# Standardisation of the second graph layer: x in pieces of 2, 4, 8 and 12 tiles, and the order of the mean's sum

## The reference, cut to what matters

```python
def _L1_gnn_ref(node_feats, adj_matrix, W, b):
    adj = adj_matrix + jnp.eye(n, dtype=adj_matrix.dtype)
    deg = jnp.sum(adj, axis=1)
    dinv = jnp.where(deg > 0, deg ** (-0.5), 0.0)
    adj_norm = dinv[:, None] * adj * dinv[None, :]
    x = node_feats @ W.T + b
    mean = jnp.mean(x, axis=0, keepdims=True)
    std = jnp.std(x, axis=0, ddof=1, keepdims=True)
    x = (x - mean) / (std + 1e-06)
    return adj_norm @ x

x = x + _L1_gnn_ref(_layernorm(x, axis=-1), adj, L1_gnn_W, L1_gnn_b)
```

## Time and profile before

| | |
|---|---|
| median of three runs | 1944.17 us |
| profiled execution | 1942.8 us |
| its span, first to last instruction | 1941.0 us |
| mean granted TensorE clock | 0.973 |
| TensorE busy | 1790.1 us (92%) |
| VectorE busy | 1619.5 us (83%) |
| ScalarE busy | 1327.9 us (68%) |
| GpSimd busy | 964.0 us (50%) |
| standardisation, first load issued | 828.90 us from the span's start |
| mean read by VectorE | 875.24 us |
| first matmul of the contraction | 879.57 us |

### The profile page before, as it was taken

One profiled execution on the slowest core, in us unless ns is written; L12 is line 12 of the kernel. 1 busy time (PEld: TensorE's weight loads), 2 busy tenths in 40 slices (PEclk: granted clock), 3 DMA queues, 4 the chain that ended last, 5 costly groups with the idle time before them and its releaser, 6 DMA issues. The chain is left out here.

```text
span 1941.0 us, 41693 instructions
## 1 busy us (share of the span) xinstructions
PE 1790.1 (92%) x12628; PEld 1683.5 (87%) x12628; DVE 1619.5 (83%) x4235; ACT 1327.9 (68%) x2651; POOL 964.0 (50%) x1703
## 2 busy tenths in 40 slices
PE   5789999739999999869999979999999999999997
PEld 4578999739999999857888869999999999999997
DVE  5799877639999999748665559999999999999996
ACT  4334555326666666444555459999999999999995
POOL 2000145535555555440101127777777777777774
PEclk9999999859999999979999999999999999999999
DMA  8776779147888888443656400000000000000002
GB/s 295 245 257 196 220 197 203 59 145 229 238 230 228 233 236 236 115 166 118 196 171 203 136 12 2 2 2 2 2 2 2 2 2 2 2 2 2 2 2 72
DMA packets 97235, 226.26 MB, mean 117 GB/s; under 512 B 20897, under 2 KB 51363, under 8 KB 88620
## 3 DMA queue, kind: packets, MB, share of 16 engines
q1 hardware_dynamic: 82476, 206.33, 34.1%
q0 software_dynamic: 14592, 17.91, 4.8%
HBM read 204.43 MB, written 19.75 MB: 115 GB/s over the span
## 5 line engine op out<-in xcount | busy, mean ns | idle before, releaser
L2036 PE MATMUL ffn_psH<-ffn_w2h,ffn_vTh 128*128 128x256 f32 x1320 | 391.8, 297 | 1.5 <-DVE ffn_u L2092 1.5
L2036 PE MATMUL ffn_psH<-ffn_w2h,ffn_vTl 128*128 128x256 f32 x1320 | 373.2, 283 | 0.0
L2036 PE MATMUL ffn_psH<-ffn_w2l,ffn_vTh 128*128 128x256 f32 x1320 | 372.8, 282 | 0.0
L2125 POOL TENSOR_SCALAR ffn_vn<-ffn_vn,ffn_rstd,ffn_shift 128x256 f32<-128x256 f32 x540 | 299.8, 560 | 21.1 <-issue 1.2
L2080 DVE BATCH_NORM_STATS2 ffn_stats<-ffn_vn 128x6 f32<-128x256 f32 x780 | 285.2, 408 | 25.1 <-ACT ffn_vn L2062 24.0
L2092 DVE SCALAR_TENSOR_TENSOR ffn_u<-ffn_th,ffn_psH 128x512 f32<-128x512 f32 x390 | 264.3, 678 | 7.3 <-ACT ffn_th L2059 7.3
L2036 PEld LDWEIGHTS ffn_psH<-ffn_w2h,ffn_vTh 128*128 128x128 f32 x1320 | 252.1, 191 | 2.5 <-DVE ffn_u L2092 1.7
L2036 PEld LDWEIGHTS ffn_psH<-ffn_w2l,ffn_vTh 128*128 128x128 f32 x1320 | 252.4, 191 | 0.8
L2036 PEld LDWEIGHTS ffn_psH<-ffn_w2h,ffn_vTl 128*128 128x128 f32 x1320 | 251.7, 191 | 0.0
L2062 ACT ACTIVATE ffn_vn<-ffn_u 128x512 f32<-128x512 f32 x390 | 248.6, 637 | 0.8 <-DVE ffn_u L2092 0.8
L2059 ACT ACTIVATE ffn_th<-ffn_psH 128x512 f32<-128x512 f32 x390 | 232.8, 597 | 1.6 <-PE ffn_psH L1999 1.6
(11 more groups left out here) (242 smaller groups left out, 4992.1 us busy)
## 6 DMA issues: line engine op xcount, KB each, us to landing
g_raw<-in_adjt SPq DMA_DIRECT2D x168, 384.0 KB, 4.6
g_raw<-in_wide SPq DMA_DIRECT2D x78, 512.0 KB, 4.3
moe_w1raw<-in_wall SPq DMA_DIRECT2D x33, 1024.0 KB, 5.2
moe_w2raw<-in_wall SPq DMA_DIRECT2D x33, 1024.0 KB, 5.9
moe_b<-in_eb SPq DMA_DIRECT2D x33, 128.0 KB
g_raw<-in_adjl SPq DMA_DIRECT2D x14, 256.0 KB, 2.7
g_raw<-in_narrow SPq DMA_DIRECT2D x13, 256.0 KB, 2.7
xn_rows<-rt_hn SPq DMA_DIRECT2D x8, 384.0 KB, 4.4
```

What stands on the lines that cost most here:

```text
L2036: last = pe.matmul(psH[w % R][:, q * D:(q + 1) * D], a[:, w % R, q * KD + k, :], b[:, k, :], start=(k == 0 and j == 0), stop=(k == KD - 1 ...
L2125: last = pool.tensor_scalar(vn[:, t, :], vn[:, t, :], rstd[:, s:s + 1], shift[:, s:s + 1], ALU.mult, ALU.add)
```

## The change

The table of pieces becomes 2, 4, 8 and 12 tiles instead of 6, 8, 6 and 6. VectorE runs the statistics of the first three pieces ahead of all z, and those of the fourth behind z of group 1. TensorE's sum of the mean begins with the two halves of GpSimd's total and ends with the last group's two tiles; the waits move with them.

```diff
@@ -1032,7 +1032,7 @@
     def __init__(self, sb, sem, g, x_rows, w1, b1, z, squares, banks, lent):
         Q = 2
         G = NT // Q
-        LOADS = ((0, 6), (6, 14), (14, 20), (20, NT))
+        LOADS = ((0, 2), (2, 6), (6, 14), (14, NT))
         B = 3
         b = sb("std_b", [P, D])
         stats = sb("std_stats", [P, NT, 6])
@@ -1088,15 +1088,15 @@
                 dve.wait_ge(aggr_done, k + 1)
                 dve.tensor_scalar(veps[:, first:end], mv[:, first:end, 1], LN_EPS, None, ALU.add).then_inc(eps_done, 1)
 
-            statistics(0)
-            statistics(1)
+            for k in range(3):
+                statistics(k)
             dve.wait_ge(w_loaded, 32)
             for k in range(G):
                 dve.wait_ge(mm_done, k + 1)
                 dve.tensor_tensor(z[:, group(k), :], psZ[k % B], b[:].unsqueeze(1).broadcast_to([P, Q, D]),
                                   ALU.add).then_inc(z_done, 1)
-                if k in (0, 2):
-                    statistics(2 + k // 2)
+                if k == 1:
+                    statistics(3)
             dve.wait_ge(sum_done, 1)
             dve.tensor_scalar(mean[:], psM, 1.0 / N, None, ALU.mult).then_inc(mean_done, 1)
             dve.wait_ge(mean_done, 1)
@@ -1177,13 +1177,13 @@
                                              stop=(d == KD - 1))
                     last.then_inc(mm_done, 1)
 
+            pe.wait_ge(total_done, G - 2)
+            for q in range(Q):
+                pe.matmul(psM, g.ones[:], total[:, q, :], start=(q == 0), stop=False)
             pe.wait_ge(z_done, G)
             for q in range(Q):
-                pe.matmul(psM, (g.ones if q < Q - 1 else g.valid)[:], z[:, (G - 1) * Q + q, :], start=(q == 0),
-                          stop=False)
-            pe.wait_ge(total_done, G - 2)
-            for q in range(Q):
-                last = pe.matmul(psM, g.ones[:], total[:, q, :], start=False, stop=(q == Q - 1))
+                last = pe.matmul(psM, (g.ones if q < Q - 1 else g.valid)[:], z[:, (G - 1) * Q + q, :], start=False,
+                                 stop=(q == Q - 1))
             last.then_inc(sum_done, 1)
 
         def add_squares(pe, k):
```

## The result

The changed kernel took 1949.34 us (median of 7 runs, 1945.50 to 1952.54), the kernel before 1943.80 us (7 runs, 1940.29 to 1945.23). The ratio is 1.0028, with a 95% interval of 1.0017 to 1.0038: 5.5 us slower (the interval is 3.3 to 7.4 us), at the upper end of the stated range, 1943.8 to 1949.4. It lies outside the forecast's own range of 1945.2 to 1948.1, and beyond the likeliest case (+2.7) by about as much as that case itself.

The account below looks back on a forecast made before the run. TensorE was taken to bound the second graph layer, then a serial handover: 3.1 us late from the last piece, less 0.4 from the sum's order, gives +2.7 on 1944.17, so 1946.9 us; range 1943.8 to 1949.4.

Parts of the forecast that it names:

- forecast's own range: Whole kernel: +1.0 to +3.9 us, 1945.2 to 1948.1, from the unknown ends; a landing off by up to 2.8 goes beyond it.
- likeliest case: Whole kernel: TensorE's pause makes it +2.7 us slower, 1946.9 us; chance 0.52.
- What bounds the stage, and the last piece: Second graph layer: TensorE bounds it; the 12-tile piece's late statistics make TensorE wait 3.4 us, group 7's transposes 3.1 late.
- central forecast: Second graph layer: TensorE waits for the 12-tile piece, 3.1 us late, less 0.4 from the mean's sum: +2.7 us; chance 0.52.
- The head: Start of the second graph layer: first transposes at least 1.6 us earlier, but groups 3 to 6 stay; group 3 gains up to 0.6.
- Where the pieces land: Loads of x: tiles 6 to 13 again there at 839.05, shift 0, far end 2.8 us either side.
- The clock: TensorE's granted clock: a pause of 3.4 us can go either way, falling to half or staying full.
- Rival (1): TensorE behind the new pause: restarts at half clock, 1.5 to 2.7 us on top, +4.2 to +5.4 in all; chance 0.27.
- The sum: TensorE's sum of the mean: totals first, behind GpSimd's last addition, which waits for group 11's bias add; gains 0.4 us.
- The sum against the run: Whole kernel: +2.7 us on the three runs' median of 1944.17 gives 1946.9; the profiled execution would go from 1942.8 to 1945.5.

## Why the prediction was right, and where it was short

- **What bounds the stage, and the last piece.** The chain from z1 to T7 was put at 9.9 us and measured 9.90 (848.68 to 858.58); its parts were 0.61, 5.16 for the statistics, 0.09, 2.27 for the power, 0.59 for the two operations behind it and 1.18 for ScalarE's rows, each within 0.02 of the forecast but the last, which was put at 1.09; the forecast's terms add up to 9.81 and were rounded up on the way, so that the sums agree to 0.01 is luck. The pause came to 3.43 for 3.4, in front of T7 and ended by ScalarE. Moving the statistics alone takes it away and brings L back to 46.62. That was the mechanism of the central forecast, and it is shown.
- **The head ("costs nothing, gives nothing").** This step was mis-sized by +0.92: T7 was forecast 30.0 after the first load (858.9 less 828.90) and came at 30.92. T3 was to gain 0.6, as if M0 would come sooner. The 4-tile piece was taken to land by 837.0, 8.1 after the first load, and it did, at 8.13; but its rows then passed statistics, power and ScalarE, so T2 was at 14.48 instead of 13.49, and with it M0. T0 came 4.1 us earlier, as forecast, and that bought nothing. The four profiles of the changed kernel's pieces have T3 at 18.66 to 19.30, and the one taken here is the lowest, so +0.92 is rather the low end of this term. The step looked at groups 3 to 6 and took M0, which hangs on groups 1 and 2, as free to move ahead.
- **Where the pieces land ("I take 0, as the bytes ahead are unchanged").** The 8-tile piece came 0.68 later with the same bytes ahead. Order counts, not only bytes: 10.83 to 12.02 in the four profiles of the new pieces against 9.42 to 10.15 in three of the old ones, and 9.74 against 7.90 and 8.12 with b moved in both. So b's load isn't the reason for the difference between the orders; the small pieces' low rate goes with it, and its cause is open. All lie within the stated 2.8 of the old landing.
- **The clock.** Rival (1), given 0.27, is what this profile shows: the fall at 859.5, 1.73 lost, inside the 1.5 to 2.7. In one thing it differs: TensorE restarted at full level, and the fall came 0.9 to 1.4 us into T7's work. The unread products give 1.68 of it back. The Trainium skill's warning on gaps between matmul bursts ("TensorE: Matmul & The Clock Gate", section "Why this matters for your kernels") agrees with the trace here, with 1.7 us as its price; the 4.07 us of the first layer had made it look less likely than it was. That pause was an exception: over the ten profiles the same pause is 2.44 to 4.83 us long, and the clock falls in it or within a microsecond behind it in eight; only in the kernel before (4.07) and in the changed kernel (2.51) it doesn't. The pauses of 3.43 in the changed kernel and 3.42 in the run with b late both ended in a fall, and so did all eight of 4.36 ahead of the contraction without unread products. As far as the profiles show, 0.27 was too low. How often it falls in the runs without a profile is open: of them only a mean is known.
- **The sum.** -0.4 forecast, -0.38 and -0.39 measured. Its cover was as said: GpSimd's last addition waited for z11. Take the late z away, as with two pieces of 6, and the same order loses about 1.1 against the old one.
- **The sum against the run.** 2.7 + 0.92 + 1.73 = 5.35, and L grew by 5.36. The median's +5.5 fits that; the terms behind the mean (-0.9, +1.2) are the clock's scatter, and together nearly nothing. The central forecast's +2.7 lies below the measured interval (3.3 to 7.4): what came is that forecast, rival (1) and a head that cost where nothing was put. The chances had 0.69 for a difference within 3.9 us and 0.27 for a larger loss, which is what the medians show. The number came inside the stated range by 0.06 us, because the range reached up to rival (1); with runs from 1945.50 to 1952.54 that is luck, and the mechanism is not.

## What to carry to other kernels

When a stream is cut into unequal pieces, the chain behind the largest one must fit into the work that the consumer still holds when its turn comes; a small first piece buys nothing if the consumer then stops in the middle. Ask of each serial step where it stands in its engine's program, not only how long it takes: the same 12 statistics cost 5 us behind z1, 1.7 of them by the clock, and nothing to be seen ahead of z0. A pause of the matmul engine can have a second price in its clock, to be added as a term of its own, and a reorder that gains because another engine is done early becomes a loss as soon as that engine's cover is gone.

## What the runs showed of the hardware that was not expected

- A load of one 1 KB row to 128 partitions brought the transfers down to 44 GB/s for a microsecond and to 119 for the next; with it moved behind the pieces three microseconds of the same stretch moved 252 GB/s instead of 108, and what followed landed 1.1 us sooner. On the old pieces the second piece was there at 9.42 to 10.15 with b ahead (three profiles) and at 7.90 and 8.12 with b behind.
- The granted clock can fall after TensorE has already restarted: at 859.5 to 860, 0.9 us or more into the work, and at 883.5 to 884, around the contraction's first matmul. A pause's price can so show on the instructions behind it, not in it.
- The length of a pause alone doesn't tell whether the clock falls: in the first graph layer it fell with one of 2.44 us and did not with one of 4.07.
- The same 14 tiles are there 1.8 us later in pieces of 2, 4 and 8 than in pieces of 6 and 8, with b behind in both (9.74 and 7.90).
